# Convolution groups of a one-core kernel as a pipeline: step 3 and norms between half stages, two places for inputs and pads

## The chip, the cores and the metric

One core of a Trainium2 chip runs the whole program. The metric is the device time of one execution, in microseconds. The engines are TensorE (PE; PEld is its weight load), VectorE (DVE), ScalarE (ACT), GpSimd (POOL) and SyncE (SP, which only issues transfers here).

## The reference, cut to what matters

x has 16 images of 32 x 32 positions with 128 channels, all float32; that is M = 16384 tokens of 128.

```python
x = x + conv(ln_c(x))            # ln_c: normalise each token, eps 1e-6
t = x as tokens
t = t + ffn(ln_t(t))             # ln_t: normalise each token, eps 1e-5

def conv(x):                     # A starts as x; each scan writes into A
    4 times: A[..., 32*i:32*i+32] = A @ w1 + b1        # step 1, 1x1
    A = relu(A)
    4 times: A[..., 32*i:32*i+32] = conv3x3(A, w2) + b2  # step 2
    A = relu(A)
    128 times: A[..., i] = A @ w3 + b3                 # step 3
    return A + x
```

The feed-forward part first computes graph attention over 524288 edges and one loop per token: edges are grouped by destination, the values of the source tokens (4 scores and 16 features, made from `ln_t(t)`) are gathered, and a softmax per destination gives gates for the two best of four experts. Each expert is 128 -> 256 -> 128 with gelu.

## The kernel before, in words

The tokens go through the convolution part in four groups (`GROUPS`) of four images, 32 tiles of 128 tokens, or eight chunks of 512. Steps 1 and 3 are each folded into one 128 x 128 matrix (`E1`, `T3`) by `small_weights` (L947). Each group has five phases, on PE at L666 to L670 and on ACT at L807 to L826:

- `token_stats` (L938, DVE): mean and variance of 32 tiles, a root on ACT (`roots`, L803), scales by DVE.
- `norm_step1` (PE L587, ACT L756): per chunk ACT normalises into `Y` and rewrites x in place as x times (1 + scale) + shift, PE transposes, ACT copies to `YT`, PE multiplies by `E1`, ACT writes the relu into the padded activations `A1`.
- `convolution` (PE L628): four stages i. A stage is two halves of 9 taps x 4 images. Stages 0 to 2 write 32 channels that the next stage reads, so ACT rewrites `A1` (L816) between them; after every stage ACT puts the relu into `XT` (L822). `Z` and `hidden_out` take turns as output.
- `step3` (PE L651): per chunk four matmuls by `T3` and four one-row matmuls that add the bias, into `MB[j % 2]`; DVE adds the result to x (L1147) and takes statistics (L1150). A bank is free for the next chunk but one when DVE has added it.
- `norm_nodes` (PE L602, ACT L782): normalise, transpose, copy to `XT` (which the feed-forward part reads later), multiply by `node_w`, copy to `node_out`.

There is one place for x (`XG`), for the padded activations (`ARENA_A`), and one set of scales. SP (L380 to L389) stores x1 and the nodes of a group, and loads x of the next one when the store has landed and ACT has read x for the last time. At the start SP issues x of group 0, the edges (two transfers of 2 MB), 23 small weights, and two stores of 20 MB that zero `payload`.

DVE's order is written out by hand (L1135 to L1154). Beside its part of the groups it makes sort keys of the edges (`make_keys`) and sorts them: `split_keys` (L1032, 23 steps over 4096 columns and a count, which frees the second halves of `KB` and `KC`), then `sort_keys(0)` (L1075) on half of the columns, 156 steps. In levels 6 and 7 a `quadrant_step` (L1066) asks POOL's queue for four transfers (`swap_quadrants`, L328), yields, and waits for them. `STEPS[g]` says how many steps come ahead of the residual chunks of group g and behind their normalisation. `sort_steps` beyond the last step do nothing.

Behind the groups come `totals`, the transposition of list 0's keys on PE (L701), their evacuation by ACT (L847) and `sources` on DVE (L1164). POOL then waits for the sources and for the nodes of all groups (L516, L517; two stores of 16 counts per group) and begins its gathers: `gather_rows` (L470), 1024 indirect transfers at L478 in all, with `gather_windows` between them and the slot gathers (L566) behind. Meanwhile PE and ACT compute the experts, DVE sorts list 1, and at the end DVE combines attention and experts.

## Time and profile before

| what | us |
|---|---|
| median of 3 runs (2850.57 to 2858.71) | 2852.92 |
| the profiled execution, its own time | 2850.96 |
| its span, first to last instruction | 2848.9 |
| PE busy | 1380.4 (48%) |
| DVE busy | 1939.1 (68%) |
| ACT busy | 675.9 (24%) |
| POOL busy | 1417.8 (50%) |

The span is that of the instructions alone; the execution's own time has 2.1 us around it. Busy time counts instructions, not waits. The granted TensorE clock is given as a share of 2.4 GHz. Over the span it is 0.69 in the mean.

### The profile page before, as it was taken

To read this page: it belongs to the slowest core of one execution; us is meant where nothing else is said; L and a number is where in the kernel's file an instruction comes from. 1 tells how busy PE (TensorE), PEld (TensorE's weight loads), DVE (VectorE), ACT (ScalarE), POOL (GpSimd) and SP (SyncE) were. 2 spreads that over 40 slices of the span, in tenths; PEclk is the share of its full clock that TensorE was granted. 3 is DMA by queue.
4 is the path that set the end of the run, shared out by engine and by line. 5 is a ranking of instruction groups with operands and counts; after the bars stand their busy time and mean duration, and the time that the engine had idled before them with its cause. 6 is when DMAs were issued, how large, how long until landed. Compare 5 with 4: busy or idle time off the path is not lost. (4 is left out here: it accounts for less than half of the span.)

```text
span 2848.9 us, 19310 instructions
## 1 busy us (share of the span) xinstructions
PE 1380.4 (48%) x6406; PEld 753.7 (26%) x6406; DVE 1939.1 (68%) x2972; ACT 675.9 (24%) x1125; POOL 1417.8 (50%) x1282
## 2 busy tenths in 40 slices
PE   2757578388387799950002370000074555455640
PEld 0225126125323555520001240000042332233320
DVE  4992884795686509999998724940137648765877
ACT  3412442431441333310001120000032313232320
POOL 1000000000000178878778777877677777777772
PEclk9965685595586599975556675555586776777765
DMA  9803101301301422220111214151243454345534
GB/s 359 338 0 36 30 1 30 35 1 30 35 16 30 51 73 77 72 47 12 14 14 44 70 46 40 18 36 15 27 126 111 160 170 153 89 157 172 156 93 124
DMA packets 192961, 221.38 MB, mean 78 GB/s; under 512 B 82202, under 2 KB 167838, under 8 KB 179294
## 3 DMA queue, kind: packets, MB, share of 16 engines
q1 hardware_dynamic: 104094, 119.66, 14.3%
q0 software_dynamic: 45888, 52.77, 10.3%
q10 hardware_dynamic: 42880, 47.73, 5.6%
q8 instruction: 50, 0.82, 0.1%
q14 instruction: 49, 0.40, 0.0%
HBM read 107.01 MB, written 106.76 MB: 75 GB/s over the span
## 5 line engine op out<-in xcount | busy, mean ns | idle before, releaser
L478 POOL DMA_INDIRECT KC<-node_dram,KB x1024 | 1142.1, 1115 | 439.7 <-issue 317.7
L680 PE MATMUL hidden_out<-XT,W 128*128 128x512 f32 x512 | 277.4, 682 | 658.3 <-ACT ARENA_A L831 657.5
L335 POOL DMA_DIRECT2D KB<-KA x8 | 4.1, 522 | 800.7 <-DVEq L1070 800.7
L680 PEld LDWEIGHTS hidden_out<-XT,W 128*128 128x128 f32 x512 | 95.8, 215 | 817.7 <-ACT ARENA_A L831 783.5
L688 PEld LDWEIGHTS Z<-W,ARENA_A 128*128 128x128 f32 x2048 | 272.2, 214 | 112.7 <-issue 112.7
L688 PE MATMUL Z<-W,ARENA_A 128*128 128x128 f32 x2048 | 298.2, 306 | 0.0
L831 ACT ACTIVATE ARENA_A<-hidden_out,b1c 128x512 f32<-128x512 f32 x256 | 174.1, 687 | 443.8 <-issue 309.3
L685 PE MATMUL Z<-b2r,ones 1*128 1x512 f32 x256 | 163.4, 721 | 147.7 <-ACT ARENA_D L839 122.8
L1028 DVE TENSOR_TENSOR KC<-KA 128x1024 f32<-128x1024 f32 (+1 forms) x196 | 199.4, 1018 | 4.9
L1029 DVE TENSOR_TENSOR KC<-KA 128x1024 f32<-128x1024 f32 (+1 forms) x196 | 198.5, 1013 | 0.0
L1231 DVE TENSOR_TENSOR KA<-XG,thresholds 128x3072 bf16<-128x3072 f32 x24 | 80.6, 3358 | 157.5 <-DMA XG<-keys_dram,win_i 156.7
L1028 DVE TENSOR_TENSOR KA<-KC 128x1024 f32<-128x1024 f32 (+1 forms) x182 | 180.5, 992 | 4.3
L1029 DVE TENSOR_TENSOR KA<-KC 128x1024 f32<-128x1024 f32 (+1 forms) x182 | 179.5, 987 | 0.0
L646 PE MATMUL hidden_out<-ARENA_A,cw 128*32 128x512 f32 x1152 | 142.3, 657 | 37.1 <-ACT ARENA_A L816 37.1
L839 ACT ACTIVATE ARENA_D<-Z 128x512 f32<-128x512 f32 x128 | 75.2, 596 | 338.5 <-PE Z L688 325.2
L625 PE MATMUL TA<-ident,ARENA_Y 128*128 128x128 f32 x256 | 68.4, 420 | 168.1 <-ACT ARENA_Y L752 167.6
L1449 DVE SCALAR_TENSOR_TENSOR XG<-XT,KB,XG 128x128 f32<-128x128 f32 x512 | 144.1, 347 | 3.7
L646 PE MATMUL Z<-ARENA_A,cw 128*32 128x512 f32 x1152 | 133.6, 624 | 21.7 <-ACT ARENA_A L816 18.6
L1346 DVE TENSOR_SCALAR KB<-XG 128x16 f32<-128x16 f32 (+1 forms) x33 | 6.0, 182 | 182.3 <-DMA KC<-payload,slot_idx 95.6
L660 PE MATMUL MB<-T,XT 128*128 128x128 f32 x256 | 101.8, 501 | 53.0 <-DVE XG L1147 34.5
L1232 DVE TENSOR_REDUCE KC<-KA 128x16 f32<-128x3072 bf16 x32 | 107.3, 3354 | 1.1
L752 ACT ACTIVATE ARENA_Y<-XG,shift,rstd 128x128 f32<-128x128 f32 x256 | 104.9, 489 | 8.6 <-DVE shift L936 8.6
(293 smaller groups left out, 2160.6 us busy)
## 6 DMA issues: line engine op xcount, KB each, us to landing
payload<-XT SPq DMA_DIRECT2D x2, 20480.0 KB
ye_dram<-ARENA_D ACTq DMA_DIRECT2D x32, 1024.0 KB, 4.2
XT<-ye_dram SPq DMA_DIRECT2D x32, 1024.0 KB, 12.2
KC<-node_dram,KB POOLq DMA_INDIRECT x1024
payload<-KC SPq DMA_DIRECT2D x132, 80.0 KB, 1.7
x_dram<-XG SPq DMA_DIRECT2D x4, 2048.0 KB, 8.7
XG<-x_dram SPq DMA_DIRECT2D x32, 256.0 KB, 9.1
out_dram<-XG ACTq DMA_DIRECT2D x32, 256.0 KB, 3.2
```

The lines of the kernel that those rows point to most:

```text
L478: pool.indirect_dma_start(row_buf[0][h][:, t, :], None, node_dram, bass.IndirectOffsetOnAxis(ap=KB[:, col:col + 1].bitcast(I32), axis=0)). ...
L646: last = pe.matmul(conv_out(i)[QUAD * q:QUAD * (q + 1), half, :], cw2[:, t, :], A1[:, q, y0:y0 + IMG_H // 2, dx:dx + IMG_W], start=t == 0, ...
L660: pe.matmul(MB[j % 2][:, t * P:(t + 1) * P], XT[:, tok:tok + P], T3[:, :], start=True, stop=False, skip_group_check=True)
L680: pe.matmul(PF[m % 2][:, :], W1[:, m // 2, (m % 2) * P:(m % 2) * P + P], XT[:, n * CHUNK:(n + 1) * CHUNK], start=True, stop=True).then_inc ...
L685: pe.matmul(Z[:, t % 2, :], ones[0:1, :], b2r[:, :], start=True, stop=False, skip_group_check=True)
L688: last = pe.matmul(Z[:, t % 2, x_ * C:(x_ + 1) * C], HH[:, 2 * x_ + kk, t * P:(t + 1) * P], W2[:, 2 * x_ + kk, :], start=False, stop=True, ...
L752: last = act.activation(Y[n % 2][:, t, :], x_tiles[:, tt, :], ACT.Identity, scale=rstd[:, tt:tt + 1], bias=shift[:, tt:tt + 1])
L831: act.activation(HH[:, m, :], PF[m % 2][:, :], ACT.Gelu, bias=b1c[:, m:m + 1]).then_inc(S["hid_out"], 1)
L1028: tt(part(dst, d, 0), part(src, d, 0), part(src, d, 1), ALU.max if d else ALU.min)
L1029: last = tt(part(dst, d, 1), part(src, d, 0), part(src, d, 1), ALU.min if d else ALU.max)
L1232: window_link(red(found[:, :, j:j + PAIR_J].rearrange("p c j -> p j c"), below, AX.X, ALU.add))
L1449: last = stt(tail_x[j][:, t, :], mine[:, t, x_ * C:(x_ + 1) * C], gate_g[:, j * TPC + t, x_:x_ + 1], tail_x[j][:, t, :], ALU.mult, ALU.add)
```

## The change

Every number of the computation stays. What changes:

- x has a place of its own in each group: `XG`, `ARENA_D`, the third quarter of `XT`, and for group 3 the second halves of `KB` and `KC` (two transfers). The padded activations have two places by turns, `ARENA_A` and the end of `XT`, which grows by 528 columns. The relu of stages goes to `relu_of[g]`. Scales of the first norm are kept twice, those of the second norm apart from them.
- SP issues x of group 0, then the weights, then the edges, then x of groups 1 and 2, then the zeros. x of group 3 is loaded when x1 of group 0 is stored and `split_keys` has counted.
- PE runs the half stages in order (`conv_half`), and behind each of the eight it does `STEP3_FILL[g][place]` step-3 chunks of the group before and `NORM_FILL[g][place]` norm chunks, in the order `NORM_ORDER`, which mixes first norms (kind 1) and node norms (kind 2). Banks are taken in the order of use. The bias of step 3 is one 512-column matmul per chunk.
- ACT's order is written out likewise: `rewrite`, norm chunks, `relu`, norm chunks, with the roots and the first two norms of a run at given places.
- DVE's order: statistics of group 0 ahead of the small weights; sort steps now also between the residual chunks (`STEPS_AFTER`).
- POOL has one more memset, and waits for the node stores alone; those of `adst` have their own semaphore, for which ACT waits later.

```diff
-STEPS = [(23, 3), (44, 8), (44, 8), (44, 8)]
+STEP3_FILL = ((0, 0, 0, 0, 0, 0, 0, 0), (2, 4, 2, 0, 0, 0, 0, 0), (2, 4, 2, 0, 0, 0, 0, 0), (2, 2, 2, 2, 0, 0, 0, 0))
+NORM_FILL = ((0, 2, 0, 2, 0, 2, 2, 0), (0, 0, 0, 3, 3, 3, 3, 4), (0, 0, 0, 3, 3, 3, 3, 4), (0, 0, 0, 0, 0, 2, 3, 3))
+NORM_ORDER = tuple((kind, g, c) for kind, g in ((1, 0), (1, 1), (1, 2), (2, 0), (1, 3), (2, 1), (2, 2), (2, 3))
+                   for c in range(CHUNKS))
+
+STEPS_AFTER = ((0, 2, 1, 1, 1, 2, 1, 0), (0, 4, 1, 1, 1, 4, 1, 0), (0, 4, 0, 4, 0, 4, 0, 0), (0, 1, 1, 1, 1, 1, 1, 0))
...
+        x_parts = [[XG[:, :]], [ARENA_D[:, 0:TILES * C]], [XT_of[2]], [KB[:, LROW:], KC[:, LROW:]]]
...
+        relu_of = [XT_of[0], XT_of[1], XG[:, :], ARENA_A[:, 0:TILES * P]]
+        late_pads = XT[:, (GROUPS - 1) * TILES * P:]
+        A1 = [(ARENA_A[:, :], late_pads)[g % 2].rearrange("p (i a b) -> p i a b", i=IMGS, b=PADW)
+              for g in range(GROUPS)]
...
             for g in range(GROUPS):
                 sp.wait_ge(S["x1_ready"], CHUNKS * (g + 1))
-                sp.dma_start(x1_groups[g], x_tiles).then_inc(S["x1_stored"], 16)
+                move_x(g, x1_groups[g], x1_stored, True)
+                if g == 0:
+                    sp.wait_ge(S["counted"], 1)
+                    move_x(GROUPS - 1, x_groups[GROUPS - 1], x_in, False)
                 sp.wait_ge(S["node_out_done"], CHUNKS * (g + 1))
                 sp.dma_start(node_groups[g], node_out[:, :, 0:WIDTH]).then_inc(S["node_stored"], 16)
-                sp.dma_start(adst_groups[g], node_out[:, :, WIDTH:]).then_inc(S["node_stored"], 16)
-                sp.wait_ge(S["x1_stored"], 16 * (g + 1))
-                sp.wait_ge(S["y_ready"], 2 * CHUNKS * (g + 1))
-                if g + 1 < GROUPS:
-                    sp.dma_start(x_tiles, x_groups[g + 1]).then_inc(S["x_in"], 16)
+                sp.dma_start(adst_groups[g], node_out[:, :, WIDTH:]).then_inc(S["adst_stored"], 16)
...
-            pool.wait_ge(S["node_stored"], 32 * GROUPS)
+            pool.wait_ge(S["node_stored"], 16 * GROUPS)
...
+            def conv_half(g, i, half):
+
+                if half == 0:
                     if i == 0:
                         pe.wait_ge(S["a1_out"], CHUNKS * (g + 1))
...
                     else:
                         pe.wait_ge(S["rewritten"], g * 12 + 4 * i)
...
+                    if 4 * g + i >= 2:
+                        pe.wait_ge(S["relu_out"], 4 * (4 * g + i - 1))
...
+            def step3(g, c):
+
+                pe.wait_ge(S["relu_out"], g * 16 + 12 + c // (CHUNKS // IMGS) + 1)
+                bank = next_bank((3, g, c), S["x1_ready"], g * CHUNKS + c + 1)
+                pe.matmul(bank[:, :].rearrange("p (t c) -> p t c", c=C), ones[0:1, :], bc(b3_row[:, :], 1, [1, TPC, P]),
+                          start=True, stop=False, skip_group_check=True)
+                for t in range(TPC):
+                    tok = (c * TPC + t) * P
+                    last = pe.matmul(bank[:, t * P:(t + 1) * P], relu_of[g][:, tok:tok + P], T3[:, :],
+                                     start=False, stop=True, skip_group_check=True)
+                last.then_inc(S["step3_ready"], 1)
...
+            norm_chunks(CHUNKS)
+            last_chunk()
             for g in range(GROUPS):
...
+                chunks = iter(range(CHUNKS))
+                for place in range(8):
+                    conv_half(g, place // 2, place % 2)
+                    if place == 0 and g >= 2:
+                        last_chunk()
+                    for c in islice(chunks, STEP3_FILL[g][place]):
+                        step3(g - 1, c)
+                    norm_chunks(NORM_FILL[g][place])
+                if g == 0:
+                    last_chunk()
+            last_chunk()
+            for c in range(CHUNKS):
+                step3(GROUPS - 1, c)
+            norm_chunks(CHUNKS)
+            last_chunk()
...
+            root1(0)
+            first_norms(1, 0)
+            norm_chunks(CHUNKS // 2)
+            root1(1)
+            norm_chunks(CHUNKS // 2)
+            last_chunk()
             for g in range(GROUPS):
...
+                if g == 0:
+                    first_norms(1, 1)
+                if g >= 2:
+                    last_chunk()
                 for i in range(4):
...
                     if i < 3:
...
+                        rewrite(g, i)
+                    elif g < 2:
+                        root1(g + 2)
+                    if (g, i) == (3, 2):
+                        first_norms(2, 2)
+                    norm_chunks(NORM_FILL[g][2 * i + 1])
+                    if (g, i) == (0, 3):
+                        last_chunk()
+                    relu(g, i)
+                    if i == 0 and 1 <= g < 3:
+                        first_norms(1, g + 1)
+                    if i == 1 and g:
+                        root2(g - 1)
+                    if i < 3:
+                        norm_chunks(NORM_FILL[g][2 * i + 2])
+            last_chunk()
+            root2(GROUPS - 1)
+            first_norms(2, GROUPS - 1)
+            norm_chunks(CHUNKS)
+            last_chunk()
...
+            def residual(g):
+
+                for c in range(CHUNKS):
+                    j = g * CHUNKS + c
+                    dve.wait_ge(S["step3_ready"], j + 1)
+                    dve.wait_ge(S["xres_ready"], j + 1)
+                    tt(x_chunk(g, c), x_chunk(g, c), MB[bank_of[(3, g, c)]][:, :], ALU.add).then_inc(S["x1_ready"], 1)
+                    dve.wait_ge(S["x1_ready"], j + 1)
+                    for t in range(TPC * c, TPC * (c + 1)):
+                        last = dve.bn_stats(bn[:, t, :], x_tile(g, t))
+                    sort_steps(STEPS_AFTER[g][c])
                 link(last)
...
+            token_stats(0)
+            scales1(0)
             small_weights()
...
+            token_stats(1)
+            keys = make_keys()
+            next(keys)
+            scales1(1)
+            next(keys)
+            token_stats(2)
+            sort_steps(11)
+            scales1(2)
+            residual(0)
+            sort_steps(5)
+            scales2(0)
+            sort_steps(24)
+            token_stats(3)
+            sort_steps(14)
+            scales1(3)
+            residual(1)
+            sort_steps(8)
+            scales2(1)
+            sort_steps(35)
+            residual(2)
+            sort_steps(8)
+            scales2(2)
+            sort_steps(19)
+            residual(3)
+            scales2(3)
+            sort_steps(ROW)
             totals()
```

## Rows read from the trace of the kernel before

**Rows 1.** Waits of POOL over the whole span: who waited for whom, total, times, longest
```profile
POOL KC L478 <- DMA adst_dram<-node_out: 118.9, 1, 118.9
...
POOL KC L478 <- DMA payload<-KC: 2.8, 1, 2.8
```

**Rows 2.** Timeline of the hand-over to the gathers: start, us, what, idle before
```profile
970.91 0.36 SPq L384 DMA_DIRECT2D node_dram<-node_out  x1
...
976.81 1.23 DVE L1164 TENSOR_SCALAR KB<-KB 128x2048 int32<-128x2048 int32 x1 [2.36 <-ACT KB L847]
...
986.95 5.88 POOL L478 DMA_INDIRECT KC<-node_dram,KB  x1 [118.93 <-DMA adst_dram<-node_out]
```

**Rows 3.** Windows of DVE alone: stretch, length, busy, PE clock, DMA share, GB/s
```profile
0.00:978.05 978.05, 695.57 (x1182) 0.71 0.26 71
93.97:209.65 115.68, 114.77 (x95) 0.77 0.30 124
306.00:402.67 96.67, 95.25 (x154) 0.82 0.00 1
862.00:907.20 45.20, 37.67 (x28) 0.69 0.09 24
```

**Rows 4.** Windows: PE, PEld, DVE, ACT, POOL busy (x), PE clock, DMA share, GB/s
```profile
0.00:971.20 971.20, 630.91 (x3404) 323.24 (x3405) 691.95 (x1166) 335.28 (x633) 14.05 (x26) 0.71 0.25 71
...
430.00:470.00 40.00, 40.00 (x112) 27.53 (x111) 10.91 (x35) 0.00 (x0) 0.00 (x0) 0.50 0.00 1
...
390.00:400.00 10.00, 10.00 (x96) 3.00 (x92) 9.86 (x17) 0.00 (x0) 0.00 (x0) 1.00 0.00 0
```

**Rows 5.** Waits of DVE from 0 to 990 us
```profile
DVE XG L1147 <- PE MB L662: 105.8, 26, 4.2
DVE bn L941 <- DMA XG<-in_x_dram: 79.2, 3, 38.4
DVE KC L952 <- PE TA L576: 31.0, 1, 31.0
DVE KA L1073 <- DMA KB<-KA: 14.1, 2, 7.2
...
DVE KA L1073 <- DMA KB<-KC: 7.0, 1, 7.0
```

**Rows 6.** Timeline of DVE, one residual chunk of group 0
```profile
222.08 0.69 DVE L1147 TENSOR_TENSOR XG<-XG,MB 128x512 f32<-128x512 f32 x1 [4.19 <-PE MB L662]
222.80 0.87 DVE L1150 BATCH_NORM_STATS2 bn<-XG 128x6 f32<-128x128 f32 x4
```

**Rows 7.** DMA issue of group 0's x: timeline, and issues with time to landing
```profile
0.88 0.88 SPq L347 DMA_DIRECT2D XG<-in_x_dram  x1
...
XG<-in_x_dram SPq DMA_DIRECT2D x1, 0.5 KB, 10.2
```

**Rows 8.** Timelines of PE and then of ACT: norm and convolution of group 0
```profile
58.07 2.07 PE L599 MATMUL MB<-ARENA_Y,E 128*128 128x512 f32 x2 [0.91 <-ACT ARENA_Y L772]
...
85.26 15.66 PE L646 MATMUL Z<-ARENA_A,cw 128*32 128x512 f32 x144 [0.79 <-ACT ARENA_A L778]
105.57 18.64 PE L646 MATMUL hidden_out<-ARENA_A,cw 128*32 128x512 f32 x144 [4.65 <-ACT ARENA_A L816]
...
70.30 1.66 ACT L752 ACTIVATE ARENA_Y<-XG,shift,rstd 128x128 f32<-128x128 f32 x4
...
74.42 1.67 ACT L752 ACTIVATE ARENA_Y<-XG,shift,rstd 128x128 f32<-128x128 f32 x4
...
100.99 4.53 ACT L816 ACTIVATE ARENA_A<-Z,cb 32x1024 f32<-32x1024 f32 x4 [15.78 <-PE Z L646]
```

**Rows 9.** Groups of PE instructions, 0 to 975 us: busy, mean ns, idle before
```profile
L646 PE MATMUL hidden_out<-ARENA_A,cw 128*32 128x512 f32 x1152 | 142.3, 657 | 37.1 <-ACT ARENA_A L816 37.1
L646 PE MATMUL Z<-ARENA_A,cw 128*32 128x512 f32 x1152 | 133.6, 624 | 21.7 <-ACT ARENA_A L816 18.6 <-ACT ARENA_A L778 3.1
...
L662 PE MATMUL MB<-b_row,ones 1*128 1x128 f32 x256 | 101.4, 497 | 0.0
```

More of the change, by code:

```diff
@@ L666, in _ @@
-            for g in range(GROUPS):
-                norm_step1(g)
-                convolution(g)
-                step3(g)
-                norm_nodes(g)
+                    if 4 * g + i >= 2:
+                        pe.wait_ge(S["relu_out"], 4 * (4 * g + i - 1))
+                for t, (dy, dx) in enumerate(TAPS):
+                    y0 = half * (IMG_H // 2) + dy
+                    for q in range(IMGS):
+                        last = pe.matmul(conv_out(i)[QUAD * q:QUAD * (q + 1), half, :], cw2[:, t, :],
+                                         A1[g][:, q, y0:y0 + IMG_H // 2, dx:dx + IMG_W],
+                                         start=t == 0, stop=True, skip_group_check=True)
@@ new lines, in _, with norm_chunks, last_chunk @@
+            transposed, used = iter(range(NORMS)), iter(range(NORMS))
+            def norm_chunks(count):
+                for n in islice(transposed, count):
+                    transpose_chunk(n)
+                    if NORM_ORDER[n] not in ((1, 0, 0), (1, 2, 0), (1, 3, 0), (2, 2, 0), (2, 3, 0), (1, 1, 0)):
+                        use_chunk(next(used))
+            def last_chunk():
+                use_chunk(next(used))
+            norm_chunks(CHUNKS)
+            last_chunk()
+            for g in range(GROUPS):
+                chunks = iter(range(CHUNKS))
[8 more added lines that the diff above has]
+                    last_chunk()
@@ L803, in roots @@
-            def roots(n):
-                act.wait_ge(S["var_ready"], n + 1)
-                act.activation(std[:, :], std[:, :], ACT.Sqrt).then_inc(S["std_ready"], 1)
+                if kind == 1:
+                    for t in range(TPC):
+                        tt = TPC * c + t
+                        last = act.activation(x_tile(g, tt), x_tile(g, tt), ACT.Identity,
+                                              scale=scale1x[g % 2][:, tt:tt + 1], bias=shift[:, tt:tt + 1])
+                    last.then_inc(S["xres_ready"], 1)
@@ new lines, in copy_chunk @@
+            def copy_chunk(n):
+                kind, g, c = NORM_ORDER[n]
+                act.wait_ge(S["yt_ready"], n + 1)
+                if kind == 1:
+                    before = sum(k == 1 for k, _, _ in NORM_ORDER[:max(n - 1, 0)])
+                    if before:
+                        act.wait_ge(S["step1_ready"], before)
+                    act.activation(YT[n % 2], TA[n % 2][:, :], ACT.Copy).then_inc(S["yt_out"], 1)
+                else:
+                    if g == 2 and c == 0:
+                        act.wait_ge(x1_stored[2], 16)
+                    act.activation(XT_of[g][:, c * CHUNK:(c + 1) * CHUNK], TA[n % 2][:, :], ACT.Copy
+                                   ).then_inc(S["yt_out"], 1)
@@ new lines, in relu @@
+            def relu(g, i):
+                act.wait_ge(S["conv_stage"], g * 4 + i + 1)
+                if (g, i) == (1, 0):
+                    act.wait_ge(S["zeros_stored"], 16 * (LISTS + 1))
+                if (g, i) == (2, 0):
+                    act.wait_ge(x1_stored[0], 16)
+                for q in range(IMGS):
+                    act.activation(relu_of[g][QUAD * i:QUAD * (i + 1), q * IMG_H * IMG_W:(q + 1) * IMG_H * IMG_W],
+                                   conv_out(i)[QUAD * q:QUAD * (q + 1), :, :].rearrange("p h n -> p (h n)"),
+                                   ACT.Relu, bias=cb2[QUAD * q:QUAD * (q + 1), :]).then_inc(S["relu_out"], 1)
@@ new lines, in _, with norm_chunks @@
+            copied, out = iter(range(NORMS)), iter(range(NORMS))
+            def norm_chunks(count):
+                for n in islice(copied, count):
+                    kind, g, c = NORM_ORDER[n]
+                    copy_chunk(n)
+                    if c or (kind, g) in ((2, 0), (2, 1)):
+                        chunk_out(next(out))
+                    if c < CHUNKS - 2:
+                        norm(n + 2)
+                    elif c == CHUNKS - 1 and (kind, g) in ((1, 2), (1, 3)):
+                        norm(n + 1)
+                        norm(n + 2)
```

307 lines of the change are left out of this document (135 added, 172 removed).

## The prediction

> **What bounds the kernel now.** I read the waits of each engine first. GpSimd (POOL) waits once for 118.9 us, on the store of node values ahead of its first gather at L478; its next longest wait on another engine's work or a transfer behind that is 2.8 us, on a payload store [rows 1]. So from the first gather at 986.95 us [rows 2] to the end at 2848.9 POOL never stands still for long, and the end follows the start of that queue one for one. What counts is when the first gather can start. The hand-over [rows 2] shows its two conditions: the sources of list 0 (L1164, started 976.81, 1.23 us long) and the store of group 3's nodes, issued in two parts from 970.91 on and landed at 987. The second was later by 9 us.
>
> Next, what fills the time ahead of it. VectorE (DVE) is busy 695.6 us of the 978.05 us to the sources [rows 3]; TensorE (PE) is busy 630.9 and ScalarE (ACT) 335.3 us of 971.2 [rows 4]. None is full: they take turns. DVE's waits say where: 105.8 us for step 3 (a chunk comes every 5.8 us, DVE uses 1.6 of it), 79.2 us for the next group's x, 31.0 us for the weights, 21.1 us for quadrant swaps [rows 5]; the chunk's times are in [rows 6]. The same four phases (norm, convolution, step 3, nodes) follow each other in all four groups.
>
> **The change, by DVE's chain.** DVE keeps every operation: the steps of list 0 are 179 before (the old list allows 182) and after (162 up to the last residual chunk, 17 behind it), statistics, keys and residual adds are the same. So I take its busy time plus its small gaps, and then count every wait that is left. Gaps: 1.42 us in a 96.67 us stretch of pure sort steps [rows 3], 1.5%, so 10 us on 695.6: 706 us. The waits after the change:
> - Start 11.1 us: x of group 0 is issued at 0.9 and lands 10.2 later [rows 7]. The statistics now stand ahead of the small weights, which took 31.0 us to come behind 4 MB of edges; they now go ahead of the edges on SP's queue. DVE is done with the statistics at 20; I leave 3 us for the weights (0 if they land by 23, 10 if the small rows, not the edges, were the slow part), and 2.5 us for the first root with its table load.
> - Edges, then x of groups 1 and 2 (two new DMAs of 2 MB), follow on the same queue ahead of the 41 MB of zeros. They move the zeros later by some 10 us; the first to need them done is ACT's relu of group 1, past 180 us. No cost. Group 3's x (two DMAs) waits on SP for the counts (about 257 us by the sum below) and is used after 24 more sort steps, 61 us; a 2 MB transfer took 10.2. No cost; without that cover it would be some 10 us.
> - Scales of group 2 wait for a root that ACT does in the last stage of convolution 0: 3 us (0 to 8).
> - First residual chunk. DVE reaches it at 11 + three statistics 26 + weights 9 + keys 43 + scales 3 + 11 steps 55 (split steps are 115.7 us for 23 [rows 3]) + the waits above = 156 us. PE: norm of group 0 starts about 35 and has ACT's pace, 4.12 us a chunk [rows 8], to 67. A stage is 15.7 to 18.6 us; between stages ACT rewrites for 4.5 us and a filler's copy and matmul (2.07 us) [rows 8] come behind it: 7.3 us. Four stages of 17.5, three gaps and the odd filler end at 164, last chunk 166. Half a stage is 7.8, with 2.6 for the restart of the clock (the stage of 18.6 us lost 3.0 against the one of 15.7) 10.4; a step-3 chunk 4.6 (below): 181. DVE waits 25 us (10 to 40).
> - Chunks inside the four residual passes: now one to four sort steps of 2.6 us (37 in 96 us [rows 3]) stand between them, 4.7 us in group 0. DVE needs 4.2 us or more a chunk in most places, PE 4.6. I take 10 us for 32 chunks (0 to 35) in place of 105.8.
> - Swaps: three waits of 7 us become two, since one request falls ahead of the last chunk and the scales: 14 us (7 to 21).
> - Totals and key evacuation: 3.5 us (the evacuation by PE and ACT takes 7, half of it beside DVE's own small work; the old wait for the totals goes, as nodes now end before the sort).
>
> Sum: 706 + 11 + 2.5 + 3 + 3 + 25 + 10 + 14 + 3.5 = 778 us for the end of the sources, against 978.05. Is the node store earlier? Behind the last residual chunk DVE still has 17 steps: 45.2 us for the last 16 of such a stretch [rows 3], 12 for what stood behind it, 57 in all, and 7 for evacuation. Nodes need 25 us (they took 947 to 971) and the store 16. So the 9 us by which the store was late go too, and POOL starts at 778 in place of 987: **209 us less**. The profiled execution took 2850.96, 2 us under the median of 2852.92; the forecast is 2643 against the former.
>
> **Does PE keep up?** A step-3 chunk has eight 128-column records and eight of the bias. The bias has 101.4 us [rows 9], 3.2 a chunk; one wide matmul replaces it. As a 128x512 matmul it takes at most the 2.07 us shown [rows 8], nearer 1.7 in a row, so a chunk falls from 5.8 to about 4.6 us. From the last step-3 chunk of one group to the first of the next PE has five half stages (52 us), five fillers of two to four chunks (46), two rewrites (6) and half a stage, a bank and a chunk (17): 121 us. DVE has 135 us of its own in the first such place and 138 in the second (43 steps each, with statistics and scales), and PE is a few us ahead when they begin, so it is some 20 us early for groups 1 and 2, but only 9 us early for group 3: there ACT's first norms wait for DVE's scales (615 us), and relu and step 3 stand behind two fillers, 667 against DVE's 676. That is the thinnest cover. Behind ACT's wait for group 3's scales (343 to 368 us) stand its rewrites, and behind them PE; it waits there for DVE's chunks anyhow. The second memset of pads costs POOL 4 us at the start, beside all.
>
> **The clock.** In the step-3 phase PE is busy 40.0 of 40 us and its granted clock is 0.50, that is 1.2 GHz; a full stretch of the convolution just before has 1.00 [rows 4]. So I price step 3 and nodes at 1.2 GHz and give each half stage a restart. The Trainium skill (TensorE: Matmul & The Clock Gate, "What's actually happening") says that the gate follows how busy the engine has been; a TensorE that is never idle would then stay at 2.4 GHz, a chunk would be 2.3 us, and the first-chunk and residual waits would be 11 us less, 2632. By that rule, the trace does not agree in this phase.
>
> **Rivals.**
> 1. PE becomes the bound: fillers leave the clock at 1.2 GHz in the half stages too. PE's 630.9 us less 47 of bias is 584. The convolutions are 275.9 us [rows 9], 8.6 a half; at 1.2 GHz 15.4, 218 more. With start 35, rewrites 40 and store 20 that is 897: 2761 us. Halfway, about 830: 2694. For it: a chunk of step 3 is slow even on a busy engine. Against: a stage after a gap of 4.65 us lost only 3.0 us against the first [rows 8]. Chance 0.17.
> 2. The pipeline holds for inputs alone: DVE no longer waits for x (79) and weights (20 of 31), but PE and DVE go on taking turns in step 3, because banks are freed in order: 99 us less, 2752. Chance 0.05.
> 3. The gain shrinks behind the first gather, since POOL's windows catch up with DVE. It loses at most the 9 us by which POOL now starts closer to DVE: 2652. Inside the forecast.
> 4. Slower: ACT's queue is in order, and every filler chunk (4.1 us on ACT) now stands between a rewrite and a relu. If each half stage runs at 1.2 GHz and PE and ACT never overlap, a group is 123 (halves) + 82 (PE's fillers) + 83 (ACT) = 288 us; four are 1152, and the first gather comes at about 1190: 3054. It decides from 233 us a group ((987 - 35 - 20) / 4). Chance 0.03. No difference: 0.02.
>
> **Chances and range.** The forecast has 0.73, its own range 2610 to 2685: all low ends of the waits together would give 38 us less (15 of the first chunk, 10 of the residuals, 7 of the swaps, 6 of weights and scales), all high ends 59 more (15, 25, 7 and 12), and they hardly fall together. To hold 8 in 10 it reaches into rival 1: 2608 to 2712. Faster by over 0.3% (what a measurement of this kernel can tell from nothing): 0.95; the same 0.02; slower 0.03.
>
> **What would show it.** First gather near 778 us, right behind the sources, and the node store well before. POOL's wait ahead of it would be on DVE. DVE busy the same 695 us before it; its wait for x gone, its wait for step 3 near 35 us. Group periods near 180 us after the first. PE's mean clock ahead of the gather above 0.71. Wrong would be: DVE idle by more than 110 us before the gather; PE busy over 650 us there; or any long wait of POOL after its start.

## The result, and the profile after

The changed kernel takes 2614.40 us (median of 4 runs, 2613.74 to 2617.11) against 2852.34 us for the kernel before on the same chip (4 runs, 2850.57 to 2858.71): ratio 0.9164, interval 0.9148 to 0.918. The prediction said 2643, so it lies inside the range of 2608 to 2712 and is 29 us faster than foreseen. The chip that ran the first four experiments was disturbed behind the first gather (the kernel before took 3256.88 us there), so of those four, which took 2911.60, 3051.49, 3079.28 and 3128.87 us, I compare only the part up to the first gather.

Read the hand-over first, as in [rows 2]. Timeline of the changed kernel: start, us, what, in brackets the idle time before it and who ended it.

```profile
713.54 0.36 SPq L423 DMA_DIRECT2D node_dram<-node_out  x1
...
753.68 1.23 DVE L1314 TENSOR_SCALAR KB<-KB 128x2048 int32<-128x2048 int32 x1 [2.59 <-ACT KB L954]
...
755.19 1.74 POOL L514 DMA_INDIRECT KC<-node_dram,KB  x1 [58.34 <-DVE KB L1314]
```

The gather starts at 755.19 in place of 986.95, 231.8 us earlier, and it is 1.74 us long in place of 5.88 [rows 2], 4.1 us less. Together 235.9 us, and the span fell by 236.2 us (2848.9 to 2612.7). So nothing was won or lost behind the first gather. POOL now waits there for VectorE's sources, not for the node store, which was issued 41.7 us before.

The waits of POOL in the changed kernel, for [rows 1]: no wait on other work behind that one is longer than 3.2 us.

```profile
POOL KC L514 <- DVE KB L1314: 58.3, 1, 58.3
```

The waits of DVE from 0 to 790 us in the changed kernel, for [rows 5]:

```profile
DVE KA L1214 <- DMA KB<-KA: 14.0, 2, 7.1
DVE bn L1038 <- DMA XG<-in_x_dram: 11.2, 1, 11.2
DVE XG L1077 <- PE MB L685: 8.1, 2, 7.6
DVE bn L1038 <- DMA ARENA_D<-in_x_dram: 6.1, 1, 6.1
DVE KB L1314 <- ACT KB L954: 2.6, 1, 2.6
DVE KC L1077 <- PE MB L685: 2.4, 1, 2.4
DVE KC L1097 <- PE TA L615: 2.2, 3, 0.7
DVE scale L1055 <- ACT std L853: 1.6, 1, 1.6
DVE KC L1090 <- PE TA L612: 1.2, 1, 1.2
```

The windows of the changed kernel, first of DVE alone up to the first gather (for [rows 3]), then of all engines (PE, PEld, DVE, ACT, POOL, clock, DMA share, GB/s; for [rows 4]):

```profile
0.00:754.91 754.91, 692.46 (x1178) 0.77 0.34 94
```

```profile
0.00:742.00 742.00, 505.15 (x3213) 224.23 (x3213) 682.80 (x1157) 336.27 (x633) 17.93 (x27) 0.77 0.34 94
```

DVE is idle for 62.4 of 754.9 us, where it was idle for 282.5 of 978.05. It is the bound now: 92% busy up to its last operation ahead of the gather. PE is busy 505 us where it was busy 631, for the same convolutions, because its step-3 work got shorter and its granted clock rose from 0.71 to 0.77 in the mean.

The groups of PE instructions, 0 to 755 us, for [rows 9] (busy, mean ns, idle before):

```profile
L671 PE MATMUL hidden_out<-XT,cw 128*32 128x512 f32 x576 | 71.4, 653 | 0.0
L671 PE MATMUL hidden_out<-ARENA_A,cw 128*32 128x512 f32 x576 | 69.2, 637 | 0.0
L671 PE MATMUL Z<-XT,cw 128*32 128x512 f32 x576 | 67.4, 624 | 1.2 <-ACT XT L839 0.8 <-ACT XT L862 0.4
L671 PE MATMUL Z<-ARENA_A,cw 128*32 128x512 f32 x576 | 66.9, 622 | 0.8 <-ACT ARENA_A L839 0.8
...
L681 PE MATMUL MB<-b_row,ones 1*128 1x512 f32 x64 | 50.0, 870 | 62.3 <-DVE XT L1077 32.3 <-DVE KB L1077 14.9 <-DVE ARENA_D L1077 11.5
```

The convolution matmuls are 274.9 us (275.9 before), and their wait for ACT, 58.8 us before [rows 9], is 2.0. The bias is 50.0 us in place of 101.4. At step 3 PE now waits for DVE in all four groups, 62.3 us together (3.6 of them in group 0, the rest as listed). DVE waits for PE there in groups 0 and 3 alone, 8.1 and 2.4 us.

How fast a chunk of step 3 is depends on what PE did before. Timeline of PE in the changed kernel, group 0:

```profile
165.93 7.93 PE L671 MATMUL Z<-XT,cw 128*32 128x512 f32 x72
173.79 1.12 PE L681 MATMUL MB<-b_row,ones 1*128 1x512 f32 x2
...
175.93 1.12 PE L681 MATMUL MB<-b_row,ones 1*128 1x512 f32 x2
...
183.85 2.04 PE L681 MATMUL MB<-b_row,ones 1*128 1x512 f32 x2 [3.58 <-DVE XG L1077]
185.82 2.08 PE L685 MATMUL MB<-T,XT 128*128 128x128 f32 x8
```

Behind a half stage without a gap a chunk is 2.14 us (173.79 to 175.93). Behind a gap of 3.58 us it is 4.0 (183.85 to 187.83). The windows of the same stretch show the clock: PE is busy all the time in each, at 1.00 (2.4 GHz) before the gap and 0.50 (1.2 GHz) behind it.

```profile
175.00:180.00 5.00, 5.00 (x27) 3.24 (x28) 4.93 (x9) 4.87 (x6) 0.00 (x0) 1.00 0.00 0
185.00:190.00 5.00, 5.00 (x22) 2.38 (x24) 4.93 (x6) 4.30 (x12) 0.00 (x0) 0.50 0.00 0
```

A gap is not needed for the fall. In group 1 the four matmuls by `T3` of the second chunk behind a half stage take 2.08 us and not 1.16, with PE busy without a break since 321.0 (timeline of PE, changed kernel):

```profile
333.78 1.12 PE L681 MATMUL MB<-b_row,ones 1*128 1x512 f32 x2
334.83 2.08 PE L685 MATMUL MB<-T,XT 128*128 128x128 f32 x8
```

By these times about half of the 32 chunks ran at full pace. The eight of group 3 all ran at 1.2 GHz.

### The profile page after: what moved, and what is told of

The parts are those of the page before. It is cut to its first block and busy times, and to the rows that moved or that the text cites. A ratio compares the mean times of both kernels' runs of the same rounds, so it can differ in the third digit from the quotient of the medians.

```text
span 2612.7 us, 19030 instructions
## 1 busy us (share of the span) xinstructions
PE 1248.0 (48%) x6214; PEld 651.3 (25%) x6214; DVE 1937.2 (74%) x2968; ACT 676.8 (26%) x1125; POOL 1417.9 (54%) x1283
## 3 DMA queue, kind: packets, MB, share of 16 engines
q0 software_dynamic: 45888, 52.77, 11.4%
## 5 line engine op out<-in xcount | busy, mean ns | idle before, releaser
L1170 DVE TENSOR_TENSOR KA<-KC 128x1024 f32<-128x1024 f32 (+1 forms) x182 | 179.3, 985 | 0.0
L734 PEld LDWEIGHTS Z<-b2r,ones 1*128 1x128 f32 x256 | 41.6, 203 | 188.7 <-ACT ARENA_D L946 125.9
L997 ACT ACTIVATE KB<-KB 128x400 f32<-128x400 f32 x32 | 17.2, 536 | 265.5 <-DVE KB L1504 262.9
L681 PE MATMUL MB<-b_row,ones 1*128 1x512 f32 x64 | 50.0, 870 | 62.3 <-DVE XT L1077 32.3
## 6 DMA issues: line engine op xcount, KB each, us to landing
XT<-ye_dram SPq DMA_DIRECT2D x32, 1024.0 KB, 11.4
```

The source lines that it names most:

```text
L681: pe.matmul(bank[:, :].rearrange("p (t c) -> p t c", c=C), ones[0:1, :], bc(b3_row[:, :], 1, [1, TPC, P]), start=True, stop=False, skip_gr ...
L734: pe.matmul(Z[:, t % 2, :], ones[0:1, :], b2r[:, :], start=True, stop=False, skip_group_check=True)
L1170: last = tt(part(dst, d, 1), part(src, d, 0), part(src, d, 1), ALU.min if d else ALU.max)
```

## The experiments

The theory: DVE's chain sets the first gather, the gather sets the end, and what is left of DVE's waits is priced by PE's chunks. The main rivals: PE or ACT sets the pace, or the gain is that of the earlier inputs alone. "Gather" is the start of the first gather, against 755.19 in the changed kernel and 986.95 in the kernel before. Each trace is of one execution. In five kernels that are alike up to there (the changed one and the variants with longer PE, longer DVE, no steps between chunks, and earlier statistics of group 3) the first residual chunk comes at 163.90, 165.34, 165.21, 164.76 and 167.43 us. So a single trace does not tell a difference of 3 or 4 us in the gather.

**PE made longer, DVE not.** In group 2, half stages 3 to 6 are run twice; the result is the same.

```diff
+                    if g == 2 and 3 <= place < 7:
+                        conv_half(g, place // 2, place % 2, again=True)
                     conv_half(g, place // 2, place % 2)
```

> The changed kernel with four half stages of convolution done twice on TensorE in group 2 (places 3 to 6): 31.5 us more PE work, where PE later waits 32.3 us for VectorE's first residual chunk of group 2. Theory (VectorE's own chain sets the first gather, PE waits for it): the first gather moves by 0 to 4 us from 755.2, span near 2613 to 2617, and the 32.3 us wait is gone. Rival (PE with ACT sets the pace and VectorE is merely balanced with it): the first gather moves by some 31 us, span near 2644.

Gather at 759.03, 3.8 us later for 31.5 us more of PE. PE's wait for the residual pass of group 2 (32.3 us before, of XT) is down to 3.5: the added work went into it. DVE's wait at the first residual chunk, ahead of the added work, was itself 1.6 us longer in this trace (9.2 for 7.6), and the residual pass of group 1, still ahead of it, began 0.9 us later (351.05 for 350.20).

**DVE made longer, PE not.** Eight more operations of 128x2048 values ahead of the 35 steps of group 2.

```diff
             scales2(1)
+            for _ in range(8):
+                link(tt(half(KB, 0), half(KA, 0), half(KA, 0), ALU.min))
             sort_steps(35)
```

> The changed kernel with eight more VectorE operations of 2048 columns (2.3 us each, results unused) behind the scales of group 1's second norm: 18.6 us more VectorE work. Theory (VectorE's chain): first gather 18 to 19 us later (774), span near 2631, and PE's wait ahead of group 2's second pair of chunks grows from 32.3 to about 51 us. Rival (PE sets the pace): span unchanged within 4 us.

Gather at 775.00: 19.8 us later for 18.6 us more of DVE. Waits of PE in this kernel:

```profile
PE MB L681 <- DVE XT L1077: 49.6, 1, 49.6
```

The same wait was 32.3. Here too 0.9 us was there ahead of the added work (351.07 for 350.20). So added work costs its full price on DVE (18.9 for 18.6) and about a tenth of it on PE (2.9 for 31.5). That is the theory's case, not rival 1's. It was tried only in group 2, where PE had 32.3 us of margin.

**The bias of step 3 as before.** Four matmuls of one row and 128 columns a chunk (eight records in the trace) in place of one wide one.

```diff
-                pe.matmul(bank[:, :].rearrange("p (t c) -> p t c", c=C), ones[0:1, :], bc(b3_row[:, :], 1, [1, TPC, P]),
-                          start=True, stop=False, skip_group_check=True)
...
+                    last = pe.matmul(bank[:, t * P:(t + 1) * P], ones[0:1, :], b3_row[:, :],
+                                     start=False, stop=True, skip_group_check=True)
```

> The changed kernel with the old bias of step 3 (four one-row matmuls of 128 columns per chunk in place of one of 512). Theory (VectorE's chain): only group 3's chunks, where PE and VectorE have the same pace of 3.9 us and PE is at 1.2 GHz, are late: 1.9 us for each of six, 8 to 15 us in all, first gather at 763 to 770. Rival (PE sets the pace): 0.8 us a chunk at 2.4 GHz and 1.8 at 1.2 GHz, 32 chunks, 30 to 50 us. If nothing moves (under 3 us), the wide bias was no part of the gain.

Gather at 780.18, 25.0 us later, more than the theory's price. The groups of DVE's residual add in this kernel (busy, mean ns, idle before and who ended it):

```profile
L1077 DVE TENSOR_TENSOR XG<-XG,MB 128x512 f32<-128x512 f32 x8 | 5.5, 688 | 15.0 <-PE MB L685 12.5 <-issue 1.5 <-DVE KA L1170 0.8
L1077 DVE TENSOR_TENSOR ARENA_D<-ARENA_D,MB 128x512 f32<-128x512 f32 x8 | 5.5, 685 | 4.4 <-issue 3.2 <-DVE KA L1170 0.9 <-DVE shift L1058 0.2
...
L1077 DVE TENSOR_TENSOR KC<-KC,MB 128x512 f32<-128x512 f32 x4 | 2.8, 688 | 9.9 <-issue 5.8 <-PE MB L685 4.1
```

With the groups of XT (1.2) and KB (3.4) that is 33.9 us of idle time ahead of the adds, against 11.4 in the changed kernel: 22.5 of the 25.0 us. Group 3, where one sort step stands between chunks, came as priced: 13.3 us for 2.6, so 10.7 more, with 8 to 15 expected for it. The size was off because of groups 0 to 2, which had been put at nothing and add 11.8 (6.7, 4.0 and 1.1; some of group 0's is the trace's own, see above). In group 3 DVE's chunks come every 5.8 us, PE's time for a chunk of narrow matmuls at 1.2 GHz (timeline of DVE, this kernel):

```profile
681.71 0.69 DVE L1077 TENSOR_TENSOR KB<-KB,MB 128x512 f32<-128x512 f32 x1 [1.41 <-issue]
687.50 0.69 DVE L1077 TENSOR_TENSOR KB<-KB,MB 128x512 f32<-128x512 f32 x1 [1.93 <-issue]
```

In the changed kernel the same adds come every 3.9 us, at DVE's own pace. The windows of this kernel also show the clock falling with PE busy all the time:

```profile
175.00:180.00 5.00, 5.00 (x48) 1.59 (x36) 4.97 (x5) 0.58 (x1) 0.00 (x0) 1.00 0.01 3
180.00:185.00 5.00, 5.00 (x21) 3.51 (x20) 3.43 (x8) 4.90 (x5) 0.00 (x0) 0.78 0.00 0
185.00:190.00 5.00, 5.00 (x15) 3.43 (x15) 4.93 (x7) 4.90 (x8) 0.00 (x0) 0.50 0.00 0
```

The half stage ends at 179.3 and narrow matmuls follow without a gap. So the wide bias is worth up to 25 us here.

**No sort steps between the chunks.** The steps of each residual pass all stand behind it.

```diff
-STEPS_AFTER = ((0, 2, 1, 1, 1, 2, 1, 0), (0, 4, 1, 1, 1, 4, 1, 0), (0, 4, 0, 4, 0, 4, 0, 0), (0, 1, 1, 1, 1, 1, 1, 0))
+STEPS_AFTER = ((0,) * 8,) * 4
...
-            sort_steps(24)
+            sort_steps(32)
...
-            sort_steps(35)
+            sort_steps(47)
...
-            sort_steps(19)
+            sort_steps(31)
```

> The changed kernel with no sort steps between residual chunks: the 38 steps come behind the scales instead, so VectorE has the same work in another order. Theory (those steps are the cover of PE's half stages and chunks): VectorE waits for step 3 again, 10.5 us grow by one half stage or two (8 us each) in groups 0 to 2 and by 2.5 us for six chunks of group 3, 45 to 75 us in all; first gather 800 to 830. Rival (the prefetch and the fillers on PE alone bring the gain; the order inside the residual does not matter): under 10 us.

Gather at 857.60, 102.4 us later. Groups of the residual add in this kernel:

```profile
L1077 DVE TENSOR_TENSOR XG<-XG,MB 128x512 f32<-128x512 f32 x8 | 5.5, 688 | 33.2 <-PE MB L685 33.2
L1077 DVE TENSOR_TENSOR XT<-XT,MB 128x512 f32<-128x512 f32 x8 | 5.5, 686 | 25.5 <-PE MB L685 25.5
```

With ARENA_D (18.8), KC (9.6) and KB (4.3) that is 91.4 us in place of 11.4: 80.0 of the 102.4. In the timeline of DVE an add of group 0 shows what the long waits are for. It is not the chunk but the half stage of the next convolution that stands between two chunks:

```profile
176.91 0.69 DVE L1077 TENSOR_TENSOR XG<-XG,MB 128x512 f32<-128x512 f32 x1 [8.41 <-PE MB L685]
```

The half stages were in the expectation, at 8 us each and one or two to a group; group 0 has two (8.4 and 9.0 us), group 1 one (9.0), group 2 two (9.2 and 9.1). Group 3 grew by 11.3, with 15 priced. What the expectation left out is the waits of 0.5 to 2.4 us for the other chunks of groups 0 to 2, which it had priced for group 3 alone, and all that is not at the adds. Of those other 22 us, 7.4 are waits for the scales (4.8 + 2.9 at L1066, 0.3 before), and 12.7 are waits for quadrant swaps, 26.7 us for 14.0: one more swap is waited for, and one wait is 12.5. Waits of DVE in this kernel:

```profile
DVE KA L1214 <- DMA KB<-KA: 19.8, 2, 12.5
...
DVE KA L1214 <- DMA KB<-KC: 6.9, 1, 6.9
```

The last 2.2 us are DVE's own busy time (694.6 for 692.5). So the steps between the chunks carry more of the gain (102 us) than any other part that I took out alone.

**Edges ahead of the weights.** The two edge loads move up to stand right behind x of group 0, as in the kernel before.

```diff
             move_x(0, x_groups[0], x_in, False)
+            edge_rows = edge_index.rearrange("a (p f) -> a p f", p=P)
+            sp.dma_start(KA[:, :].bitcast(I32), edge_rows[0]).then_inc(S["edges_in"], 16)
+            sp.dma_start(KB[:, :].bitcast(I32), edge_rows[1]).then_inc(S["edges_in"], 16)
```

> The changed kernel with the edges (two transfers of 2 MB) again ahead of the 23 small weights on SyncE's queue. Theory: the weights land at about 31 instead of 23 us, so VectorE waits some 7 us more for them, but x of group 1 (6.1 us waited for now) is then no later than it was, so most of it is given back: first gather 2 to 8 us later than 755.2. Rival (the small rows are slow by themselves, whatever is ahead): no change of the weights' landing, under 1 us.

2631.33 us (one run), span 2629.6, gather at 770.33: 15.1 us later, about twice the upper end of what was expected. Waits of DVE in this kernel:

```profile
DVE XG L1077 <- PE MB L685: 18.0, 2, 16.8
...
DVE KC L1090 <- PE TA L612: 10.8, 1, 10.8
```

The weights come 9.6 us later (10.8 for 1.2), and the first residual chunk also waits 9.2 longer (16.8 for 7.6), while the 6.1 us for group 1's x go: 12.7 of the 15.1 us. PE's first transpose of a weight starts its whole chain, and that chain ends last at the first residual chunk. So in the first 164 us it is PE, started by the weights, that sets the time, and only behind it does DVE.

**x of groups 1 and 2 behind the zeros.**

```diff
-            for g in (1, 2):
-                move_x(g, x_groups[g], x_in, False)
...
             sp.dma_start(payload[LISTS * LIST:LISTS * LIST + SLOTS], zeros[0:SLOTS, 0:WIDTH]).then_inc(S["zeros_stored"], 16)
+            for g in (1, 2):
+                move_x(g, x_groups[g], x_in, False)
```

> The changed kernel with x of groups 1 and 2 issued behind the 41 MB of zeros in place of ahead of them. Theory (one queue in order, and VectorE's order is fixed): statistics of group 1 wait until the zeros are written, near 140 us, in place of 38.7: VectorE stands for some 100 us and the first gather comes 90 to 105 us later, span near 2710. Rival (a later start is made good, since PE and VectorE have margins behind it, or the transfers share the engines): under 50 us.

2708.83 us (one run), span 2707.1, gather at 851.14: 96.0 us later, as the theory had it, and the span is 94.4 longer. Waits of DVE:

```profile
DVE bn L1038 <- DMA ARENA_D<-in_x_dram: 103.9, 1, 103.9
```

An x that comes late is paid almost in full: the wait is 97.8 us longer (103.9 for 6.1), less 2.0 at the first residual chunk (5.6 for 7.6). The pipeline has no room for it.

**The kernel before with the wide bias alone.** The same edit as the reverse of the narrow bias above, in the old order.

> The kernel before with the wide bias matmul alone. Two readings of why step 3 stayed at 1.2 GHz on a busy TensorE: (a) the one-row matmuls count little as activity, so with half of the records gone the clock rises within the phase and a chunk falls from 5.8 to 2.2 to 3 us; (b) the gap ahead of it lowers the clock and 128-column matmuls never raise it: a chunk falls to 4.1 us only. Span: (a) 80 to 110 us less, (b) 40 to 60 us less than 2849, of which group 0's part is hidden behind the sort.

2804.80 us against 2852.96 beside it (one run each), 48.2 less. The span is 2803.1, 45.8 us less than in the trace of the kernel before. The gather is at 944.20, 42.8 earlier. Groups of DVE's residual add: first the kernel before, then this one.

```profile
L1147 DVE TENSOR_TENSOR XG<-XG,MB 128x512 f32<-128x512 f32 x32 | 21.9, 686 | 119.9 <-PE MB L662 105.8 <-issue 14.0
```

```profile
L1147 DVE TENSOR_TENSOR XG<-XG,MB 128x512 f32<-128x512 f32 x32 | 22.0, 687 | 73.9 <-PE MB L662 59.0 <-issue 14.9
```

46.0 us less idle time, and the chunk's own time in PE's timeline of this kernel (group 0):

```profile
214.16 2.07 PE L658 MATMUL MB<-b_row,ones 1*128 1x512 f32 x2
...
218.17 2.07 PE L658 MATMUL MB<-b_row,ones 1*128 1x512 f32 x2
```

A window of the same stretch (columns as for [rows 4]):

```profile
215.00:225.00 10.00, 10.00 (x26) 5.38 (x25) 3.98 (x14) 0.00 (x0) 0.00 (x0) 0.50 0.00 0
```

A chunk is 4.0 us in place of 5.8, at 1.2 GHz with PE busy all the time. So this step 3, in one piece, does not come back to 2.4 GHz with the wide bias; that is the outcome and the price of reading (b), but the reason that (b) gives is not tested. It also shows that some 46 of the 238 us are to be had without any pipeline.

**The kernel before with a semaphore of its own for the second node store.** The first gather reads the first store alone, so it need not wait for both.

```diff
-            pool.wait_ge(S["node_stored"], 32 * GROUPS)
+            pool.wait_ge(S["node_stored"], 16 * GROUPS)
```

> The kernel before with the second node store on a semaphore of its own, for which the gathers don't wait. The first gather of the kernel before took 5.88 us, that of the changed one 1.74. Theory (it queues behind the small rows of the second node store, which are landing): it starts earlier (981 to 984 in place of 987) but lasts as long as that store is in flight, 6 us or more, so the span falls by 0 to 3 us. Rival (first use of the gather's code, or something of its place): it lasts 5.9 us and all of the earlier start is gained, 3 to 6 us.

2855.82 us against 2852.96 beside it (one run each), no gain to be seen. The hand-over in this kernel's timeline:

```profile
977.21 0.36 SPq L384 DMA_DIRECT2D node_dram<-node_out  x1
...
987.87 11.26 POOL L478 DMA_INDIRECT KC<-node_dram,KB  x1 [113.51 <-DMA node_dram<-node_out]
```

The nodes were done 6.3 us later here (977.21 for 970.91). That is not the edit's hand-over: the stores of x1 (L382) of the four groups already go out 2.2, 5.5, 6.7 and 6.3 us later. Why is open. Count from that issue: the gather starts 10.7 us behind it, not 16.0, but its end is 21.9 us behind it in both kernels (987.87 + 11.26 - 977.21, and 986.95 + 5.88 - 970.91). What the wait gives up, the gather pays back. I take it that the gather's own packets stand behind those of the second store; the trace shows the lengths alone. The stores of the keys, which follow on the same queue (L418, at 980.90 here), can't be the reason alone: in the changed kernel they are issued from 750.00, 5.2 us ahead of the gather, and it takes 1.74.

**Statistics of group 3 twelve steps earlier.** PE waits once for 32.7 us on ACT in the changed kernel, from 281 to 314; that was not foreseen in this place. ACT's root for group 3 stands in its queue ahead of a copy that PE needs, and waits for DVE's statistics. Timeline of the changed kernel:

```profile
313.50 0.23 ACT L853 ACTIVATE std<-std 128x32 f32<-128x32 f32 x1 [39.00 <-DVE std L1047]
313.63 0.58 ACT L826 ACTIVATE XT<-TA 128x512 f32<-128x512 f32 x1
...
314.26 1.90 PE L655 MATMUL MB<-node_w,XT 128*128 128x24 f32 x8 [32.75 <-ACT XT L826]
```

```diff
-            sort_steps(24)
+            sort_steps(12)
             token_stats(3)
-            sort_steps(14)
+            sort_steps(26)
```

> The changed kernel with the statistics of group 3 behind 12 sort steps of the block of 24, in place of behind all 24 (26 steps then follow in place of 14). ACT's root for them stands in its queue ahead of norm chunks, and PE waits 32.7 us behind it (until 314 us) in the changed kernel. Theory (VectorE's chain sets the time, PE's idle time is margin): PE's wait of 32.7 us falls to under 5 and comes back as a wait for VectorE's first residual chunk of group 1 (5.6 us grow to some 30), the first gather stays at 755 within 1 us, span 2612 to 2614. Rival (ACT's in-order queue costs time): 5 to 30 us less.

2618.22 us (one run), gather at 758.59. The wait on ACT is gone, and came back where PE waits for DVE's adds in group 1: 34.7 us in place of 5.6. The 32.7 us had been part of PE's margin, so there is no gain. The 3.4 us by which the gather is later are the first residual chunk's wait (11.1 for 7.6), ahead of the edit.

**Three waits filled.** Signs ahead of the statistics, first key step ahead of group 1's, three sort steps ahead of the first residual chunk (taken from between the chunks); and then the same together with the edit above.

```diff
-STEPS_AFTER = ((0, 2, 1, 1, 1, 2, 1, 0)
+STEPS_AFTER = ((0, 1, 1, 1, 0, 1, 1, 0)
...
             scales1(2)
+            sort_steps(3)
             residual(0)
```

> The changed kernel with three waits of VectorE filled by its own later work: the sign bits are made while x of group 0 is under way (1.9 us), the first part of the keys (9 us) stands ahead of the statistics of group 1, which now wait 6.1 us for x, and three sort steps (14 us) stand ahead of the first residual chunk (7.6 us waited) in place of between chunks of that group. Theory (VectorE's chain): up to 15.5 us less, 8 to 15.5 with PE's start unchanged: first gather 740 to 747, time 2599 to 2606. Rival (PE's chain from its first transpose to the first residual chunk sets that part as firmly): the wait for step 3 grows by what is gained elsewhere and the gain is under 5 us.

> Both edits together: the three filled waits, and the statistics of group 3 twelve steps earlier, so that PE has margin ahead of group 1's residual chunks, which VectorE now reaches up to 15 us earlier. Theory: the first gather is at the low end, 740 to 742, up to 5 us ahead of the version without the earlier statistics, where PE's margin there was only 5.6 us. Rival (the 5.6 us are enough, as chunks 0 and 1 are ready long before): the two are the same within 1 us.

The first took 2620.43 us (median; 2612.26 to 2621.43), ratio 0.9168 (0.9146 to 0.9191); the second 2612.64 (2610.93 to 2621.55), ratio 0.9152 (0.9129 to 0.9175). Neither differs measurably from the changed kernel's 0.9164 (0.9148 to 0.918). In their profiled executions the gathers start at 750.78 and 754.08, 4.4 and 1.1 us earlier where 8 to 15.5 were expected, and the spans are 1.1 and 0.8 us shorter. That is the rival's case, a gain under 5 us. The second is 3.3 us behind the first, which neither reading of it had; its first residual chunk is 1.7 us later (169.11 for 167.40). The waits moved more than they went. DVE in the first, around the first chunks:

```profile
167.40 0.69 DVE L1077 TENSOR_TENSOR XG<-XG,MB 128x512 f32<-128x512 f32 x1 [2.24 <-issue]
...
179.54 0.69 DVE L1077 TENSOR_TENSOR XG<-XG,MB 128x512 f32<-128x512 f32 x1 [3.93 <-issue]
```

The three steps hide the wait ahead of the first chunk, but with fewer steps behind the second one DVE meets PE's half stage (3.9 us), and the signs now wait 8.9 us for POOL's constants. Of what DVE still waits for in this kernel, 8.3 us in group 0 lie against PE's own chain and 14.2 are the swaps.

## Why the prediction was right, and where 29 us came from

**What bounds the kernel: right.** The gather follows DVE's chain, and the end follows the gather one for one (231.8 + 4.1 of 236.2 us; 96.0 against 94.4 with late inputs). Lengthening DVE moved it by 19.8 for 18.6 us, lengthening PE by 3.8 for 31.5. The first 164 us are the exception: there PE's chain from the weights sets the time, and the prediction had that too, as DVE's wait at the first residual chunk.

**DVE keeps every operation, plus 10 us of gaps: right.** 692.5 us busy (695.6 foreseen, 3.1 less); the waits listed make 49.4 of the 62.4 idle us, so gaps are 13.0 (3.0 more).

**The first residual chunk, 25 us: this is the term that was mis-sized.** It measured 7.6. DVE was there at 156.3, as foreseen (156), but the chunk came at 163.90 and not at 181. PE's chain to it was 17 us shorter than priced, and most of that lay ahead of step 3 (timeline of PE, changed kernel):

```profile
61.85 15.66 PE L671 MATMUL Z<-ARENA_A,cw 128*32 128x512 f32 x144 [0.78 <-ACT ARENA_A L839]
...
153.78 7.93 PE L671 MATMUL Z<-XT,cw 128*32 128x512 f32 x72 [0.78 <-ACT XT L839]
```

The convolution of group 0 began at 61.85 and not at 67. Its stages took 65.8 us and not 70, its gaps and fillers 2.7 less than priced, so that the half stage behind it began at 153.78 and not at 166. That is 12.2 of the 17 us. The half stage took 7.9 us, priced at 10.4 with a restart of the clock, and the step-3 chunk 2.14, priced at 4.6: 5.0 us. The prediction's "I price step 3 and nodes at 1.2 GHz and give each half stage a restart" accounts for these 5.0 and for the 4.2 of the stages; the other 8 us are an early start and shorter gaps.

What the clock did: in the old step 3, one piece of 40 us and more, it is 0.50 [rows 4]. In pieces of two or three chunks right behind a half stage it is mostly 1.00, falls behind gaps, and fell once without one (334.83). The eight chunks of group 3 stand at 0.50. Of the two values weighed in the prediction, the one by the Trainium skill (TensorE: Matmul & The Clock Gate, "What's actually happening", a gate that follows how busy the engine has been) was 2632. The 2.14 us chunk agrees with its 2.3. But the kernel with the narrow bias has the clock falling from 1.00 to 0.50 in three windows that are each 5.00 of 5.00 us busy, so busy time as the profile counts it does not tell the clock by itself.

**Inside the residual passes, 10 us: too high.** It measured 2.9 (the other 0.5 us of L1077's XG, and 2.4 at the last chunk of group 3). A chunk was priced at 4.6 us against DVE's 4.2. It took 2.14 at full clock, and at 1.2 GHz 4.0, which is what DVE needs in group 3 (3.9). Together with the first chunk: 10.5 for 35, 24.5 us of the miss.

**Small terms.** Start 11.2 (11.1 foreseen); swaps 14.0 (14); weights 1.2, with 2.2 for their transposes behind (3); root 1.6 (2.5); scales of group 2 none (3); evacuation 2.6 (3.5). "No cost" for the order of inputs missed 6.1 us: group 1's x comes behind the edges and DVE was there first, at 32.7. The 706 of busy time and gaps was 705.5, and the start was summed as 11. Sum of the terms: -24.5 + 0.4 + 6.1 - 3 - 0.9 - 0.9 - 0.5 + 0.2 = -23.1, which is 778 less 754.9, the end of the sources. Another 4.1 us are the shorter first gather, which the prediction did not look for: it counted the late store as lost starting time (9 us) but not in the gather's own length. The rest of the 29 us is mostly rounding: 209 off the profiled 2850.96 is 2642, where the prediction wrote 2643.

**The node store: right.** Issued 713.54; with the 16 us of before it has landed at 730, and the sources are done at 754.9.

**Does PE keep up: right in the result, wrong in the margins.** The first chunk of step 3 was to be ready 20, 20 and 9 us ahead of DVE in groups 1, 2 and 3. It was ready at 333.8, 486.4 and 642.6 for adds that begin at 350.20, 527.92 and 660.73: 16, 42 and 18 us early. Behind its first two chunks PE then waits 5.6, 32.3 and 14.9 us. The thinnest cover was group 1 and not 3, since ACT's root for group 3 held PE for 32.7 us ahead of it. The prediction followed ACT's wait for the scales of group 3, but not the root ahead of them: put between two copies, it waits for DVE's statistics.

**The signs that were named.** Gather near 778 (755), wait for it on DVE, wait for x nearly gone (6.1), step 3 below 35 (10.5), mean clock above 0.71 (0.77). The residual passes begin at 163.90, 350.20, 527.92 and 660.73: periods of 186, 178 and 133 us. Near 180 for two; the last is shorter, as only 19 steps and no statistics stand there. None of the three signs of a wrong theory is there: DVE idle 62, PE busy 505, POOL's longest later wait 3.2.

**The rivals.** PE as the bound falls with the two lengthened kernels, for all but the first 164 us. The gain of inputs alone (2752) falls with the result itself: it would have kept the 105.8 us that DVE waited for step 3, and 10.5 are left. The variants show what each part holds: 102 us are lost without the steps between chunks, 96 with the inputs of groups 1 and 2 behind the zeros (one wait of 103.9 us, where the kernel before had three that make 79.2), 25 with the narrow bias. These overlap and needn't add up. A loss behind the first gather is excluded by the spans. The slower case wanted a group of over 233 us; the longest period is 186. A slip in rival 1, on which nothing hangs: halfway between 778 and 897 is 838, not 830.

## What to carry to other kernels

Price each wait of a pipeline by what stands on the other engine's queue between its two ends, a half stage or a root, and not by the item that is waited for: with no sort steps between the chunks a 2 to 4 us chunk cost waits of 8 to 9. Where one engine is the bound, add some 20 us to each engine in turn and see which of them the end follows; a gain sought on the other only turns into its waiting. Do it in each phase, as the bound can change: here PE had margin behind 164 us and none ahead of it. A short matmul phase in pieces between dense stages can run at twice the pace of the same phase in one piece (about half of the chunks did here), so measure it there before pricing it by the old row.

## What the runs showed of the hardware

- **PE's clock with PE busy.** A long step 3 is at 0.50 with 40.00 of 40 us busy [rows 4] with the narrow bias, and with 10.00 of 10 with the wide one (5.8 and 4.0 us a chunk). The wide bias right behind a half stage ran three chunks (173.8 to 180.2) at full clock; the narrow one, behind the same half stage, had the full pace to 182.6 (pairs of 0.49 us) and then lost it (0.66, 0.80). The wide one lost it without a gap too: in group 1 of the changed kernel (334.83), and in the kernel without steps between chunks, whose chunk pieces go from 1.12 and 1.16 us to 1.89 and 2.07 at 180 to 182. What decides it I did not separate.
- **The same stage in two traces.** In the third stage of group 0's convolution the same 144 matmuls took 15.66 us in the changed kernel's trace, at 1.00, and 17.36 in those of the four variants that are alike up to there. In the one without steps between chunks the clock is 0.56 over the first 3.5 us of the stage. PE stands for 3.4 us shortly ahead of it in both, so the loss behind the same gap is not the same in each execution.
- **The first indirect gather.** It took 5.88 us 16 us behind the issue of the last node store, 4.14 us 17.8 us behind it (wide bias alone: issued 926.41, started 944.20), 11.26 us 10.7 us behind it, and 1.74 or 1.75 us in the changed kernel (41.7 us behind it) and all its variants. In all three kernels with the old pair of stores (the kernel before, its wide bias, its second semaphore) the end of the gather was 21.9 us behind the issue, whatever it had waited for.
